# Six small gate and norm operations of a mixture-of-experts block moved from VectorE to GpSimd

## The chip, the core and the metric
One core of one Trainium2 chip. The time is device microseconds for one execution of the kernel; the engines are TensorE (PE), VectorE (DVE), ScalarE (ACT), GpSimd (POOL) and the queue that issues transfers (SP).

## What is computed
A block of three layers over x of 16 sequences x 256 tokens x 128 features, in float32:

```
x = x + 0.5 * moe(layernorm(x))
x = x + attention(layernorm(x))
x = x + 0.5 * moe(layernorm(x))

def moe(x):                       # x: 4096 tokens x 128, 8 experts, top 2
    probs = softmax(x @ Wg)
    top_vals, top_idx = top_k(probs, 2)
    gates = top_vals / sum(top_vals)
    expert_out[e] = x @ We[e] + be[e]
    return sum over the two chosen e of gates * expert_out[e]
```

The attention layer (16 heads of 8 features, causal, with a cumulative log-sigmoid bias) is not touched by the change.

## The kernel before
The 4096 tokens are 32 tiles of 128, kept in SBUF as `x_all` for the whole kernel, in 8 groups of Q = 4 tiles. The kernel runs the first MoE layer over the groups, attention over 16 sequences, and the second MoE layer over the same groups. Each engine has a list of its own, written out by hand as `part(i, s, q)`: i is the step, s its static number, q the place (0 to 3) of a tile inside the group. Step s works on three groups at once: the experts of group s (condition B), the gates of group s + 1 (A) and the norm of group s + 2 (N). Steps from 2 to 5 are a loop on the engines. The last two MoE steps of the first layer and the first three of the second are interleaved with attention steps by a fixed order (`beside`), the same on all engines. Between steps -2, -1 and 0 of the first layer POOL's list has the fills and masks that attention needs (`set_up_rows`, `set_up_columns`, `set_up_masks`). Semaphores order the engines; no instruction overtakes another of its engine.

For a tile, TensorE multiplies by all 8 experts (six matmuls of 512 columns, L416 and L417, since float32 is split into high and low parts). VectorE takes experts 0 to 3 as four chained steps `lower = bank * gate + lower` (`expert`, L288), ScalarE scales experts 4 to 7 (L246, `scaled`), POOL adds them in pairs (L216 `pair`, L220 `upper`, together `add_upper`), and VectorE adds lower and upper into x (`finish`, L297). Two buffers of each alternate between tiles.

The gates of the next group take, in order:
- TensorE: the logits' twelve small matmuls in q = 1.
- VectorE: the largest values (L357) and their difference `gap` (L374), the indices of the two largest (L376).
- ScalarE: `egap` = exp(gap) (L252), followed on its list by four `xn` (L270, the normalised tiles of the group after) and the scaled tile of q = 2.
- VectorE in q = 2: `hot` (L362, which expert is the first and second choice), `denom` (L366), `g12` (L380, L396), and `hot` times `g12` (L401).
- VectorE in q = 3: `gates` (L369, sum of the two), `gates3` (L383 and L388, high and low parts).
- TensorE in q = 0 of the next step, behind its experts: transpose of `gates3` (L434); ScalarE copies it (L259, ahead of its scaled tile); TensorE multiplies it with the bias (L441); VectorE adds that to x (L340).

The norm of a group takes VectorE's L335 and L344 (`moments`), `neg_mean` (L352) and `var_eps` (L353), in q = 0, with L315 and L316 as the same two for the first two groups; then POOL's `rstd_of`: `rstd` = var_eps to the power -1/2 (L225) and `shift` (L228), behind `add_upper` of q = 0.

`chain` is a semaphore that counts VectorE's gate steps, CH of them a group; `after_link(n, k)` waits for step k.

Of the kernel before, what the change touches and what calls it, by code (L numbers as in the profile page):

```python
# [4 lines left out]
FP32 = mybir.dt.float32  # L5
# [3 lines left out]
ALU = mybir.AluOpType  # L9
# [3 lines left out]
P = 128  # L13
EPS = 1e-5
# [10 lines left out]
def wait_apart(eng, sem, value, counted):  # L25

    eng.wait_ge(sem, value)
    eng.sem_inc(counted, 1)
# [137 lines left out]
def moe_layer(nc, ctx, c, made, tiles, banks, x_all, tag, x_dram=None, out_dram=None, before=None):  # L166
# [30 lines left out]
    CH = 8  # L197
# [14 lines left out]
    def gpsimd(pool):  # L212
# [10 lines left out]
        def rstd_of(n, b):  # L223
            pool.wait_ge(eps_done, n)
            nc.gpsimd.tensor_tensor(rstd[:, b], var_eps[:, b], c["minus_half"][:, 0:Q],  # L225
                                    ALU.pow).then_inc(rstd_done, 1)
            pool.wait_ge(rstd_done, n)
            nc.gpsimd.tensor_tensor(shift[:, b], neg_mean[:, b], rstd[:, b], ALU.mult).then_inc(shift_done, 1)  # L228

        def part(i, s, q):  # L230
            N, B, b, n = s + 2 < G, 0 <= s, s % 2, i + 3
            if B:
                add_upper(i, q)
            if q == 0 and N and not (x_dram is not None and s == -1):
                rstd_of(n, b)
            if q == 0 and x_dram is not None and s == -2:
                rstd_of(2, 1)
# [39 lines left out]
    def vector(dve):  # L277
# [21 lines left out]
        def after_link(n, k):  # L299

            dve.wait_ge(chain, (n - 1) * CH + k)

        def first_groups():

            for g in range(2):
# [9 lines left out]
                nc.vector.tensor_scalar(neg_mean[:, g], moments[:, g, :, 0], -1.0, None, ALU.mult)  # L315
                nc.vector.tensor_scalar(var_eps[:, g], moments[:, g, :, 1], EPS, None, ALU.add).then_inc(eps_done, 1)  # L316

        def part(i, s, q):
            N, A, B = s + 2 < G, -1 <= s and s + 1 < G, 0 <= s
            a, b, m, n = (s + 1) % 2, s % 2, i + 3, i + 2  # L320
            flat = gates[:, a].rearrange("p q e -> p (q e)")
# [28 lines left out]
            if q == 0 and N and not early:  # L350
                dve.wait_ge(mom_done, m)
                nc.vector.tensor_scalar(neg_mean[:, b], moments[:, b, :, 0], -1.0, None, ALU.mult)  # L352
                nc.vector.tensor_scalar(var_eps[:, b], moments[:, b, :, 1], EPS, None, ALU.add).then_inc(eps_done, 1)  # L353
# [5 lines left out]
            if q == 2 and A:  # L359

                dve.wait_ge(no_ready, n)
                nc.vector.tensor_tensor(hot[:, :, :, :], every, best_no[:, :, 0:2].rearrange("p q r -> p r q").unsqueeze(3)  # L362
                                        .broadcast_to([P, 2, Q, E]), ALU.is_equal)

                dve.wait_ge(egap_ready, n)
                nc.vector.tensor_scalar(denom[:, :], egap[:, :], 2.0, 2.0, ALU.mult, ALU.add).then_inc(chain, 1)  # L366
            if q == 3 and A:
                after_link(n, 6)
                nc.vector.tensor_tensor(gates[:, a], hot[:, 0], hot[:, 1], ALU.add).then_inc(chain, 1)  # L369
# [11 lines left out]
            if q == 3 and A:  # L381
                after_link(n, 7)
                nc.vector.tensor_copy(gates3[:, 0:3:2], flat.unsqueeze(1).broadcast_to([P, 2, Q * E])).then_inc(chain, 1)  # L383
            if B:
                expert(i, s, q, 2)
            if q == 3 and A:
                after_link(n, 8)
                nc.vector.tensor_tensor(gates3[:, 1], flat, gates3[:, 0].bitcast(FP32), ALU.subtract).then_inc(gates_ready, 1)  # L388
# [10 lines left out]
            if q == 2 and A:  # L399
                after_link(n, 5)  # L400
                nc.vector.tensor_tensor(hot[:, :, :, :], hot[:, :, :, :],  # L401
                                        g12[:, :, :].unsqueeze(3).broadcast_to([P, 2, Q, E]), ALU.mult).then_inc(chain, 1)
# [676 lines left out]
```

## Time and profile before

| | |
|---|---|
| median of 3 runs | 488.97 us (486.0 to 489.73) |
| the profiled execution | 487.24 us, span from first to last instruction 485.5 us |
| TensorE matmul busy | 416.7 us (86%) |
| VectorE busy | 372.5 us (77%) |
| ScalarE busy | 278.3 us (57%) |
| POOL busy | 239.7 us (49%) |
| mean granted TensorE clock | 0.981 |

Busy time is what an engine's instructions took, without their waits; matmuls are pipelined, so a busy TensorE is not one at its peak. Shares are averages over the three layers: the first MoE layer lies at about 16 to 100 us, attention at about 80 to 405 us, the second MoE layer from about 375 us on. "Start" in the rows below is in us from the first instruction, L is the line of the kernel, and a bracket tells how long the engine was idle before and what released it.

### The profile page before, as it was taken

The page shows a single profiled execution, that of the slowest core. Times are in us where ns is not written, and L with a number is a line of the kernel's source. Part 1 is how long each engine was busy: PE and PEld are TensorE (multiplying, and loading weights), DVE is VectorE, ACT ScalarE, POOL GpSimd, SP SyncE. Part 2 cuts the span into 40 slices and gives each one's busy share as a digit, 9 for nine tenths or more (in the row PEclk, how much of TensorE's full clock was granted, in tenths as well). Part 3 has the DMA queues.
Part 4 walks back from the last instruction along what each step waited for, and adds up shares of the span by engine and source line. Part 5 has one row for each costly group of instructions (what it writes and reads, how often), then busy time and mean ns, then how long its engine had stood idle before and what let it go on. Part 6 is the DMA issues. An engine that isn't in the chain of part 4 may idle for free.

```text
span 485.5 us, 12085 instructions
## 1 busy us (share of the span) xinstructions
PE 416.7 (86%) x3472; PEld 303.6 (63%) x3488; DVE 372.5 (77%) x1316; ACT 278.3 (57%) x758; POOL 239.7 (49%) x397
## 2 busy tenths in 40 slices
PE   1888887847799999999999999999989999888884
PEld 0656566526556766676676676676667666566662
DVE  4999999874856865876785686676576658999995
ACT  5676766440354555565556466455555685666753
POOL 8955566351425534533543543553442543566554
PEclk9999999895989999999999999999999999999999
DMA  3311000033333333234233233323322000001101
GB/s 108 92 52 20 1 0 1 8 99 109 101 98 101 94 100 115 73 96 114 69 104 102 85 96 100 100 84 98 111 77 80 4 3 0 24 24 32 33 22 43
DMA packets 29402, 32.47 MB, mean 67 GB/s; under 512 B 2312, under 2 KB 26140, under 8 KB 29370
## 3 DMA queue, kind: packets, MB, share of 16 engines
q1 hardware_dynamic: 28282, 31.57, 22.1%
q10 hardware_dynamic: 1088, 0.52, 0.4%
q8 instruction: 14, 0.23, 0.2%
q14 instruction: 18, 0.15, 0.1%
HBM read 16.05 MB, written 15.20 MB: 64 GB/s over the span
## 4 chain that ended last, share of the span: by engine, by line
PE 40%; DVE 22%; DMA 19%; issue 10%; ACT 3%; POOL 3%; DVEq 1%; SPq 1%; ACTq 0%; POOLq 0%; another core or an unknown queue 0%
DMA a_q_rows<-a_max_t 16%; PE bank L847 10%; PE bank L862 7%; DVE m_lower L288 7%; PE bank L877 6%; PE bank L850 3%; PE bank L968 2%; PE bank L960 2%; PE bank L963 2%; DVE m_stats L335 2%; DMA q_stage<-a_q_parts 2%; POOL m_pair L216 2%; DVE x_all L297 2%; DVE m_best_no L376 2%; PE bank L886 1%
## 5 line engine op out<-in xcount | busy, mean ns | idle before, releaser
L773 DVE TENSOR_REDUCE a_neg_max<-bank 128x2 f32<-128x512 f32 (+1 forms) x192 | 124.3, 687 | 76.2 <-PE bank L850 70.2
L712 ACT ACTIVATE a_weights<-bank 128x512 f32<-128x512 f32 x192 | 108.4, 592 | 60.5 <-PE bank L862 55.6
L658 POOL TENSOR_SCALAR_AFFINE_SELECT a_weights<-a_weights 128x512 f32<-128x512 f32 (+1 forms) x96 | 75.7, 790 | 127.9 <-ACT a_weights L712 127.7
L847 PE MATMUL bank<-a_k_rows,a_q_rows 104*128 104x256 f32 (+1 forms) x512 | 100.9, 321 | 7.7 <-DMA a_k_rows<-k_stage 6.5
L847 PEld LDWEIGHTS bank<-a_k_rows,a_q_rows 104*128 104x128 f32 x512 | 78.9, 199 | 26.9 <-issue 18.5
L246 ACT ACTIVATE m_scaled<-bank,m_gates 128x128 f32<-128x128 f32 x256 | 72.6, 367 | 25.0 <-PE bank L417 25.0
L862 PE MATMUL bank<-a_q_rows,a_k_rows 106*128 106x512 f32 (+1 forms) x192 | 69.8, 442 | 11.1 <-DMA a_q_rows<-a_max_t 10.5
L216 POOL TENSOR_TENSOR m_pair<-m_scaled 128x256 f32<-128x256 f32 x64 | 48.3, 755 | 60.4 <-ACT m_scaled L246 60.1
L288 DVE SCALAR_TENSOR_TENSOR m_lower<-bank,m_gates,m_lower 128x128 f32<-128x128 f32 x192 | 66.1, 344 | 1.2
L877 PE MATMUL bank<-a_weights,a_v 128*32 128x128 f32 x1536 | 61.6, 279 | 0.0
L850 PE MATMUL bank<-a_mask,a_ident 128*128 128x256 bf16 (+1 forms) x176 | 56.4, 321 | 0.0
L877 PEld LDWEIGHTS bank<-a_weights,a_v 128*32 128x32 f32 x1536 | 36.1, 109 | 25.4 <-issue 20.6
L416 PE MATMUL bank<-we_hi,m_xt_hi 128*128 128x512 f32 x64 | 31.8, 497 | 13.7 <-DVE m_lower L288 13.6
L862 PEld LDWEIGHTS bank<-a_q_rows,a_k_rows 106*128 106x128 f32 (+1 forms) x192 | 29.9, 193 | 17.2 <-DMA a_q_rows<-a_max_t 10.0
L701 ACT ACTIVATE a_max_t<-bank 32x128 fp32r<-32x128 f32 x32 | 8.5, 267 | 46.7 <-PE bank L891 46.7
L220 POOL TENSOR_TENSOR m_upper<-m_pair 128x128 f32<-128x128 f32 x64 | 29.6, 462 | 5.7 <-POOL m_pair L216 1.3
L416 PEld LDWEIGHTS bank<-we_hi,m_xt_hi 128*128 128x128 f32 x64 | 12.4, 194 | 24.0 <-DVE m_lower L288 23.3
L270 ACT ACTIVATE m_xn<-x_all,m_shift,m_rstd 128x128 f32<-128x128 f32 (+1 forms) x64 | 26.4, 486 | 0.3 <-POOL m_shift L228 0.3
L417 PE MATMUL bank<-we_hi,m_xt_hi 128*128 128x512 f32 x64 | 25.8, 403 | 0.0
L417 PE MATMUL bank<-we_lo,m_xt_hi 128*128 128x512 f32 x64 | 25.8, 403 | 0.0
L416 PE MATMUL bank<-we_lo,m_xt_hi 128*128 128x512 f32 x64 | 25.7, 402 | 0.0
L417 PE MATMUL bank<-we_hi,m_xt_lo 128*128 128x512 f32 x64 | 25.7, 402 | 0.0
(126 smaller groups left out, 784.0 us busy)
## 6 DMA issues: line engine op xcount, KB each, us to landing
a_k_rows<-k_stage SPq DMA_DIRECT2D x16, 416.0 KB
k_stage<-a_k_parts SPq DMA_DIRECT2D x48, 128.0 KB
q_stage<-a_q_parts SPq DMA_DIRECT2D x48, 128.0 KB
a_q_rows<-q_stage SPq DMA_DIRECT2D x64, 96.0 KB
x_all<-in_L_attn_x SPq DMA_DIRECT2D x8, 256.0 KB, 2.8
out_x<-x_all SPq DMA_DIRECT2D x8, 256.0 KB, 2.3
we<-in_L_ffn_We SPq DMA_DIRECT2D x1, 512.0 KB, 4.0
k_stage<-a_c_parts SPq DMA_DIRECT2D x32, 16.0 KB
```

The costliest lines, as they stand in the source:

```text
L216: nc.gpsimd.tensor_tensor(pair[:, q % 2], scaled[:, q % 2, 0:2], scaled[:, q % 2, 2:4], ALU.add).then_inc(pair_done, 1)
L246: last = nc.scalar.activation(scaled[:, q % 2, j], y_high[q % 2][:, j * D:(j + 1) * D], ACT.Copy, scale=gates[:, s % 2, q, 4 + j:5 + j])
L288: nc.vector.scalar_tensor_tensor(out=lower[:, q % 2, j], in0=y_low[q % 2][:, j * D:(j + 1) * D], scalar=gates[:, s % 2, q, j:j + 1], in1=t ...
L416: nc.tensor.matmul(y_low[q % 2][:, :], x_part, w_part[:, 0:H], start=k == 0, stop=k == 2)
L417: last = nc.tensor.matmul(y_high[q % 2][:, :], x_part, w_part[:, H:2 * H], start=k == 0, stop=k == 2)
L658: nc.gpsimd.affine_select(out=diagonal, in_=diagonal, compare_op=ALU.is_ge, fill=0.0, base=0, pattern=[[0, heads.stop - heads.start], [1, P]],
L712: nc.scalar.activation(weights[n // 2 % 3][:, half:half + 4, :].rearrange("p h n -> p (h n)"), wt_bank[n % 2][:, :], ACT.Exp).then_inc(wt_ ...
L773: nc.vector.tensor_reduce(neg_max[:, t, first:first + heads], score_bank[p % 2][:, :].rearrange("p (h n) -> p h n", h=heads), AX.X, ALU.ma ...
L847: nc.tensor.matmul(bank[:, n * keys:(n + 1) * keys], q_rows[b][0:KR, h, t * P:(t + 1) * P], k_rows[b][0:KR, h % NU, 0:keys], start=n == 0, ...
L850: nc.tensor.matmul(own, ident16[:, :], mask16[:, 0:heads, :], start=False, stop=True, skip_group_check=True).then_inc(scores_ready, 1)
L862: nc.tensor.matmul(bank[:, :], k_rows[b][0:rows, u, jt * P:(jt + 1) * P], q_rows[b][0:rows, u:H:NU, t * P:(t + 1) * P], start=True, stop=T ...
L877: last = nc.tensor.matmul(out_bank[t][32 * g:32 * (g + 1), u // 2 * P:(u // 2 + 1) * P], v_sb[b][:, jt * H // 2 + 2 * g + u // 2, u % 2:u ...
```

## The change
POOL takes six operations from VectorE: `var_eps` and `neg_mean` of the norm (at the head of `rstd_of`), and `hot` times `g12`, the sum of `gates`, and the two steps of `gates3`. The four of the gates stand in POOL's list in q = 3, ahead of `add_upper` of that tile. The copy in L383 becomes an addition of 0.0. New semaphores carry the dependencies: `hot_done` from VectorE to POOL, `hot_scaled`, `gates_done` and `gates_hi_done` between POOL's steps, `neg_done` for the norm; VectorE's writing of `hot` waits for `gates_done` of the group before. L315 and L316, for the first two groups, are moved too.

```diff
--- before.py
+++ after.py
@@ -194,7 +194,9 @@
     y_ready, high_used = sem("y_ready"), sem("high_used")
     low_chain, pair_done, upper_done, upper_used = sem("low_chain"), sem("pair_done"), sem("upper_done"), sem("upper_used")
     stored, waited = sem("stored"), sem("waited")
-    CH = 8
+    neg_done, hot_done, hot_scaled = sem("neg_done"), sem("hot_done"), sem("hot_scaled")
+    gates_done, gates_hi_done, pool_waited = sem("gates_done"), sem("gates_hi_done"), sem("pool_waited")
+    CH = 5
 
     def load_group(sp, g):
 
@@ -221,14 +223,32 @@
                                     ALU.add).then_inc(upper_done, 1)
 
         def rstd_of(n, b):
+            wait_apart(pool, mom_done, n, pool_waited)
+            nc.gpsimd.tensor_scalar(var_eps[:, b], moments[:, b, :, 1], EPS, None, ALU.add).then_inc(eps_done, 1)
+            nc.gpsimd.tensor_scalar(neg_mean[:, b], moments[:, b, :, 0], -1.0, None, ALU.mult).then_inc(neg_done, 1)
             pool.wait_ge(eps_done, n)
             nc.gpsimd.tensor_tensor(rstd[:, b], var_eps[:, b], c["minus_half"][:, 0:Q],
                                     ALU.pow).then_inc(rstd_done, 1)
+            pool.wait_ge(neg_done, n)
             pool.wait_ge(rstd_done, n)
             nc.gpsimd.tensor_tensor(shift[:, b], neg_mean[:, b], rstd[:, b], ALU.mult).then_inc(shift_done, 1)
 
         def part(i, s, q):
             N, B, b, n = s + 2 < G, 0 <= s, s % 2, i + 3
+            A, a, m = -1 <= s and s + 1 < G, (s + 1) % 2, i + 2
+            flat = gates[:, a].rearrange("p q e -> p (q e)")
+            if q == 3 and A:
+                pool.wait_ge(hot_done, m)
+                pool.wait_ge(chain, (m - 1) * CH + 5)
+                nc.gpsimd.tensor_tensor(hot[:, :, :, :], hot[:, :, :, :],
+                                        g12[:, :, :].unsqueeze(3).broadcast_to([P, 2, Q, E]), ALU.mult).then_inc(hot_scaled, 1)
+                pool.wait_ge(hot_scaled, m)
+                nc.gpsimd.tensor_tensor(gates[:, a], hot[:, 0], hot[:, 1], ALU.add).then_inc(gates_done, 1)
+                wait_apart(pool, gates_done, m, pool_waited)
+                nc.gpsimd.tensor_scalar(gates3[:, 0:3:2], flat.unsqueeze(1).broadcast_to([P, 2, Q * E]), 0.0, None,
+                                        ALU.add).then_inc(gates_hi_done, 1)
+                pool.wait_ge(gates_hi_done, m)
+                nc.gpsimd.tensor_tensor(gates3[:, 1], flat, gates3[:, 0].bitcast(FP32), ALU.subtract).then_inc(gates_ready, 1)
             if B:
                 add_upper(i, q)
             if q == 0 and N and not (x_dram is not None and s == -1):
@@ -312,13 +332,10 @@
                     last = nc.vector.bn_aggr(moments[:, g, k], stats[:, k])
                 last.then_inc(mom_done, 1)
                 dve.wait_ge(mom_done, g + 1)
-                nc.vector.tensor_scalar(neg_mean[:, g], moments[:, g, :, 0], -1.0, None, ALU.mult)
-                nc.vector.tensor_scalar(var_eps[:, g], moments[:, g, :, 1], EPS, None, ALU.add).then_inc(eps_done, 1)
 
         def part(i, s, q):
             N, A, B = s + 2 < G, -1 <= s and s + 1 < G, 0 <= s
             a, b, m, n = (s + 1) % 2, s % 2, i + 3, i + 2
-            flat = gates[:, a].rearrange("p q e -> p (q e)")
             early = x_dram is not None and s < 0
 
             if early and s == -2 and q == 0:
@@ -347,10 +364,6 @@
                 if q == 0:
                     dve.wait_ge(bias_added, i + 1)
                 expert(i, s, q, 0)
-            if q == 0 and N and not early:
-                dve.wait_ge(mom_done, m)
-                nc.vector.tensor_scalar(neg_mean[:, b], moments[:, b, :, 0], -1.0, None, ALU.mult)
-                nc.vector.tensor_scalar(var_eps[:, b], moments[:, b, :, 1], EPS, None, ALU.add).then_inc(eps_done, 1)
             if q == 1 and A:
                 wait_apart(dve, logits_ready, n, waited)
                 for k in range(Q):
@@ -359,14 +372,12 @@
             if q == 2 and A:
 
                 dve.wait_ge(no_ready, n)
+                at_least(dve, gates_done, n - 1)
                 nc.vector.tensor_tensor(hot[:, :, :, :], every, best_no[:, :, 0:2].rearrange("p q r -> p r q").unsqueeze(3)
-                                        .broadcast_to([P, 2, Q, E]), ALU.is_equal)
+                                        .broadcast_to([P, 2, Q, E]), ALU.is_equal).then_inc(hot_done, 1)
 
                 dve.wait_ge(egap_ready, n)
                 nc.vector.tensor_scalar(denom[:, :], egap[:, :], 2.0, 2.0, ALU.mult, ALU.add).then_inc(chain, 1)
-            if q == 3 and A:
-                after_link(n, 6)
-                nc.vector.tensor_tensor(gates[:, a], hot[:, 0], hot[:, 1], ALU.add).then_inc(chain, 1)
             if B:
                 expert(i, s, q, 1)
             if q == 1 and A:
@@ -378,14 +389,8 @@
             if q == 2 and A:
                 after_link(n, 3)
                 nc.vector.reciprocal(g12[:, 0], denom[:, :]).then_inc(chain, 1)
-            if q == 3 and A:
-                after_link(n, 7)
-                nc.vector.tensor_copy(gates3[:, 0:3:2], flat.unsqueeze(1).broadcast_to([P, 2, Q * E])).then_inc(chain, 1)
             if B:
                 expert(i, s, q, 2)
-            if q == 3 and A:
-                after_link(n, 8)
-                nc.vector.tensor_tensor(gates3[:, 1], flat, gates3[:, 0].bitcast(FP32), ALU.subtract).then_inc(gates_ready, 1)
             if q == 3 and N:
                 dve.wait_ge(hi_ready, m)
                 nc.vector.tensor_tensor(xt_lo[:, b], xt_bank[:, :], xt_hi[:, b].bitcast(FP32), ALU.subtract).then_inc(lo_ready, 1)
@@ -396,10 +401,6 @@
                 nc.vector.tensor_tensor(g12[:, 1], egap[:, :], g12[:, 0], ALU.mult).then_inc(chain, 1)
             if B:
                 expert(i, s, q, 3)
-            if q == 2 and A:
-                after_link(n, 5)
-                nc.vector.tensor_tensor(hot[:, :, :, :], hot[:, :, :, :],
-                                        g12[:, :, :].unsqueeze(3).broadcast_to([P, 2, Q, E]), ALU.mult).then_inc(chain, 1)
             if q == 3 and s == G - 1:
                 finish(G * Q - 1, 1)
         return part
```

## Rows read from the trace of the kernel before

**Rows 1.** Stretch by engine: us, busy us (instructions), TensorE clock, DMA share, GB/s
```profile
440.00:450.00 10.00, 8.57 (x42) 6.46 (x42) 9.88 (x54) 6.85 (x24) 6.06 (x10) 1.00 0.09 26
```

**Rows 2.** VectorE in order of time (start us, us), fourth tile of a steady group
```profile
441.52 0.22 DVE L401 TENSOR_TENSOR m_hot<-m_hot,m_g 128x64 f32<-128x64 f32 x1
441.83 0.35 DVE L288 SCALAR_TENSOR_TENSOR m_lower<-bank,m_gates,x_all 128x128 f32<-128x128 f32 x1
442.09 0.34 DVE L369 TENSOR_TENSOR m_gates<-m_hot 128x32 f32<-128x32 f32 x1
442.36 0.34 DVE L288 SCALAR_TENSOR_TENSOR m_lower<-bank,m_gates,m_lower 128x128 f32<-128x128 f32 x1
442.62 0.36 DVE L383 CAST m_gates<-m_gates 128x64 fp32r<-128x64 f32 x1
442.90 0.34 DVE L288 SCALAR_TENSOR_TENSOR m_lower<-bank,m_gates,m_lower 128x128 f32<-128x128 f32 x1
443.16 0.17 DVE L388 TENSOR_TENSOR m_gates<-m_gates 128x32 fp32r<-128x32 f32 x1
443.26 0.68 DVE L391 TENSOR_TENSOR m_xt_lo<-bank,m_xt_hi 128x512 fp32r<-128x512 f32 x1
```

**Rows 3.** Weight loads in order of time, the gates' transpose [idle before, releaser]
```profile
443.39 0.12 PEld L434 LDWEIGHTS bank<-ident,m_gates 128*96 128x96 f32 x1 [0.31 <-DVE m_gates L388]
```

**Rows 4.** In order of time, from the logits' largest values: VectorE, ScalarE, POOL
```profile
437.87 0.39 DVE L357 MAX8 m_best<-bank 128x8 f32<-128x8 f32 x4
...
438.90 1.66 ACT L270 ACTIVATE m_xn<-x_all,m_shift,m_rstd 128x128 f32 x4
440.46 1.11 ACT L246 ACTIVATE m_scaled<-bank,m_gates 128x128 f32<-128x128 f32 x4
...
441.65 0.73 POOL L216 TENSOR_TENSOR m_pair<-m_scaled 128x256 f32<-128x256 f32 x1 [2.45 <-ACT m_scaled L246]
442.46 0.47 POOL L220 TENSOR_TENSOR m_upper<-m_pair 128x128 f32<-128x128 f32 x1
```

**Rows 5.** VectorE in order of time, two groups later, where it waits for TensorE
```profile
463.32 0.18 DVE L388 TENSOR_TENSOR m_gates<-m_gates 128x32 fp32r<-128x32 f32 x1
...
464.77 0.69 DVE L340 TENSOR_TENSOR x_all<-x_all,bank 128x512 f32<-128x512 f32 x1 [0.21 <-PE bank L441]
...
467.66 0.39 DVE L357 MAX8 m_best<-bank 128x8 f32<-128x8 f32 x4 [0.32 <-PE bank L449]
```

**Rows 6.** VectorE and POOL in order of time, first tile of a steady group
```profile
445.97 0.32 DVE L288 SCALAR_TENSOR_TENSOR m_lower<-bank,m_gates,x_all 128x128 f32<-128x128 f32 x1
446.21 0.40 DVE L352 TENSOR_SCALAR m_neg_mean<-m_moments 128x4 f32<-128x4 f32 x1
446.52 0.16 DVE L353 TENSOR_SCALAR m_var_eps<-m_moments 128x4 f32<-128x4 f32 x1
446.59 0.72 DVE L288 SCALAR_TENSOR_TENSOR m_lower<-bank,m_gates,m_lower 128x128 f32<-128x128 f32 x2
...
446.12 0.46 POOL L220 TENSOR_TENSOR m_upper<-m_pair 128x128 f32<-128x128 f32 x1 [0.16 <-POOL m_pair L216]
```

**Rows 7.** Groups of POOL instructions: count, busy us, mean ns, idle before, releaser
```profile
L225 POOL TENSOR_TENSOR m_rstd<-m_var_eps,minus_half 128x4 f32<-128x4 f32 x16 | 17.3, 1082 | 3.6 <-DVE m_var_eps L353 2.4 <-DVE m_var_eps L316 1.1
L228 POOL TENSOR_TENSOR m_shift<-m_neg_mean,m_rstd 128x4 f32<-128x4 f32 x16 | 3.2, 200 | 1.3
```

**Rows 8.** In order of time at the start of the kernel: POOL, VectorE, ScalarE
```profile
16.69 0.94 POOL L630 MEMSET a_ones_r<- 2x1024 f32 x1
...
20.62 0.63 POOL L648 TENSOR_SCALAR_AFFINE_SELECT a_mask<-a_mask 128x512 bf16<-128x512 bf16 x1
...
17.91 0.16 DVE L396 TENSOR_TENSOR m_g<-m_egap,m_g 128x4 f32<-128x4 f32 x1
...
24.73 1.64 ACT L270 ACTIVATE m_xn<-x_all,m_shift,m_rstd 128x128 f32<-128x128 f32 x4
```

**Rows 9.** VectorE in order of time, where the second MoE part begins beside attention
```profile
376.05 0.92 DVE L352 TENSOR_SCALAR m_neg_mean<-m_moments 128x4 f32<-128x4 f32 x1
```

## The prediction
> **What bounds the kernel now.** I read the busy shares first, then one stretch of the second MoE part, then the order of time inside one group, engine by engine, and last the first and last group and the seams with attention. Over the whole span TensorE is the busiest engine, an average that hides stages with different limits. Inside a MoE part VectorE is busy 9.88 of 10 us, TensorE 8.57 and POOL 6.06 at a full clock [rows 1], so a group of four tiles goes at VectorE's pace. The interval between groups is that between two L388: 463.32 - 443.16 = 20.16 us for two groups, 10.08 each, taken as 10.1 [rows 2, 5]. Each MoE part has one group at its start, six further gate computations in a row before or beside attention, and ten plain steady intervals in all (five a part).
>
> The question is not how much VectorE loses but what the gates hang on once POOL makes them. POOL runs its list in order. In a steady group it waits for ScalarE's scaled tile of the third tile, adds the pair at 441.65 and the upper half at 442.46, which ends at 442.93 [rows 4]. Only behind that does the change put the four gate steps. VectorE today ends them at 443.33 [rows 2], and TensorE waits for them: its weight load for the gates' transpose sat idle 0.31 us until L388 [rows 3]. So there is no slack at all at this end: what POOL delivers later, TensorE starts later.
>
> **What leaves VectorE.** I price by distance between starts, since durations overlap. L288 links wait for the one before and stand 0.38 us apart with nothing between (two of them take 0.72 us: 0.38 + 0.34 [rows 6, 2]). An operation that follows an L288 without needing it starts 0.26 behind it (442.36 to 442.62). L401 needs nothing of its neighbours and is needed by neither: its 441.52 to 441.83, 0.31 us, are all saved [rows 2]. L369: 441.83 to 442.36 is 0.53 against 0.38, saves 0.15. L383: 442.36 to 442.90 is 0.54, saves 0.16. L388: 443.16 to 443.26, saves 0.10 [rows 2]. L352 and L353: 445.97 to 446.59 is 0.62 against 0.38, saves 0.24 [rows 6]. Together 0.96 us a group: if VectorE stayed the limit, 10.1 would become 9.1.
>
> **What comes to POOL.** No row shows a tensor_scalar there. Two-input operations cost 0.20 us at 4 elements a partition [rows 7], 0.47 at 128 and 0.73 at 256 [rows 4], so about 2.1 ns an element over 0.2 or a little less. That gives 0.32 for the product of 64 elements, 0.26 for the sum of 32, 0.26 for the subtraction. The copy of 64 (a tensor_scalar) lies between 0.20 and 0.32; I take 0.25, one input being the nearer to the lower row. They are a chain with three waits on POOL's own results. Such a wait costs 0.08 us between pair and upper (442.38 to 442.46 [rows 4]); with a second semaphore and a counted threshold I take 0.12, bounds 0.08 and 0.2. The chain G is 0.32 + 0.26 + 0.25 + 0.26 + 0.36 = 1.45 us. Its floor, four operations at the 0.20 of the smallest row and three waits of 0.08, is 1.04; its ceiling, each operation held up once, about 2.0. The two norm steps add 0.20 each and their waits, some 0.6 us before rstd.
>
> **The lap that closes.** With the gates on POOL a ring runs through four engines once a group; I add it up from one end of the gates to the next.
> - Gates ready to L340 (transpose, ScalarE's copy, bias matmul): 463.32 + 0.18 = 463.50 to 464.77, where L340 did wait for TensorE: 1.27 us.
> - L340 to L357: 464.77 to 467.66, with L357 waiting for TensorE's logits: 2.89 us. Here the matmuls of one tile and twelve logits matmuls lie, not the two removed norm steps, so VectorE's saving doesn't shorten it [rows 5].
> - L357 to the end of the third tile's upper half: 437.87 (the largest values), 438.90 (four xn, behind the exponential of the gap), 440.46 (scaled tile), 441.65, 442.46, end 442.93: 5.06 [rows 4], and 0.05 to POOL's next step: 5.11 us. xn cannot start before the gap is known, as ScalarE's list has them in that order, and the scaled tile stands behind xn.
> - G, 1.45 us.
> The lap is 1.27 + 2.89 + 5.11 + 1.45 = 10.72 us, over the 10.1 of today and the 9.1 that VectorE would allow. So VectorE gives 0.96 back into idle time, mostly before L340, and each steady interval becomes 0.62 us longer: ten of them, +6.2. Even at the floor of G the lap is 10.31, +0.2 each. The norm steps lie on a branch: upper half of the first tile, norm 1.9 (0.6, rstd 1.02 to 1.08, shift 0.20, the rest waits [rows 7]), xn. By POOL's pairs behind the gates I reckon xn could start 4.9 to 5.1 us after the gates by this branch, and 5.2 by the lap above, so they cost nothing as long as G stays about where I put it; without that cover they cost their 0.6.
>
> **The ends.** At the start POOL has a long list of fills (L630 at 16.69 to L648's end at 21.25, 4.56 us) [rows 8]. They stand behind the group's fourth-tile place in POOL's list, where nothing of POOL stood until now; the gates wait for g12 (L396 ends 18.07), so the gates are ready at 19.6, the fills end at 24.2, pair and upper of the first tile at 25.5, norm at 27.4, and xn starts at 27.4 to 27.5 instead of 24.73 [rows 8]: +2.7. The next gates come behind POOL's upper half, 1.5 instead of 0.4 after it [rows 2, 4]: +1.1. Together +3.8, bounds +1 (the fills then hidden) and +5. In the second MoE the first gates are late by the same step, +0.9 (0.7 to 1.1), five intervals are in the ten, and the last, without xn in its lap, I put at +0.3. At the seams with attention VectorE is relieved: L352 took 0.92 us beside a POOL operation just ahead of a row maximum [rows 9], so -0.7 there (0 to -1.4), and -0.3 (0 to -1.0) beside the first attention steps. Attention itself, some 260 us, contains no moved instruction: 0.
>
> Sum: 3.8 + 6.2 + 0.9 + 0.3 - 0.7 - 0.3 = +10.2 us. Against the profiled execution's own 487.24 us (its span is 485.5) that is 497.4; that execution lies 1.7 us under the median of the three runs, 488.97, which would give 499.2. I take a value between the two, 498.
>
> **A rule beside the rows.** L352 took 0.40 us at 446.21 against 0.16 for its like L353, and ended at 446.61, with POOL's L220 that ended at 446.58; at the seam it took 0.92 [rows 6, 9]. The Trainium skill, "SBUF — State Buffer", section "Who interferes with whom", says that VectorE operations in a two-port mode, or with two inputs in SBUF, and POOL operations exclude one another for a whole instruction. The trace agrees. By that rule the change removes such collisions from VectorE and hands POOL four to six more operations that can be held up; the first is in my start-to-start prices, the second is the third rival.
>
> **Rivals.**
> - VectorE stays the limit and the chain is hidden: ten intervals of -0.96 and -1.0 at the seams give 476.6 us. For it speaks the 98% of VectorE. Against it, POOL ends the upper half at 442.93, and TensorE wants the gates at about 443.3: a chain of over 0.4 us is already late. It would need ScalarE to finish the scaled tile a full microsecond earlier in the group. It decides from a lap below 10.1, thus G under 0.83, where the floor is 1.04. Chance 0.1.
> - Chain at its floor, and the fills not on the path: ten times +0.2, +0.9, +0.3, -1.0, and +1 to +3 for the start: 489.5 to 492, within 1%. For it: small operations might all cost 0.20. Chance 0.18.
> - The lap lengthened by collisions: each POOL step of the chain and of the norm held up by 0.24, as L352 was; G 2.4 with the chain's four, lap 11.7, ten times +1.6 and the ends: about 507. Against: during the chain VectorE mostly reads PSUM (L288, L391). Chance 0.1.
> - My forecast, G between 1.2 and 2.0: chance 0.62, 494 to 503.
>
> **Range and chances.** A measurement of this kernel can tell a change from none from about 1%. The range 490 to 504 takes in the forecast and most of the second rival; outside stay the first, the third in part. Faster by over 1%: 0.1, the first rival. Within 1%: 0.2, the second rival and a little of the forecast's lower end. Slower by over 1%: 0.7.
>
> **What would show it.** In the changed kernel: six groups of VectorE gone and 96 POOL operations of 0.20 to 0.33 us new; gate groups 10.7 us apart; VectorE under 90% busy in a MoE stretch with idle time before L340, put down to TensorE's bias matmul; TensorE waiting for POOL's gates, no longer for VectorE's; xn of the first full group near 27 us. It is wrong if groups stand under 10.1 apart, if POOL's chain takes under 1 us, or if the fills don't delay the first pair. A granted TensorE clock that falls in MoE stretches with more idle time would lengthen the 2.89 us and make it worse than forecast.

## The result, and the profile after

The changed kernel takes 499.34 us (median of 4 runs, 497.43 to 507.1) beside 487.49 for the kernel before (4 runs, 483.54 to 489.73); the ratio is 1.024, 95% interval 1.018 to 1.030. It is slower, by 1.8 to 3.0%. One of its four runs, 507.1 us with a mean granted TensorE clock of 0.939 where the others have 0.964 to 0.984, is left out of the ratio. The profiled execution took 497.83 us, its span is 496.1 against 485.5, so 10.6 us are to be found.

The stretch of one group in the second MoE part of the changed kernel (us, busy time of TensorE, its weight loads, VectorE, ScalarE, POOL with the instructions, clock, transfers) answers to [rows 1]:

```profile
441.90:452.70 10.80, 8.63 (x42) 6.52 (x42) 9.31 (x49) 6.96 (x23) 7.50 (x17) 1.00 0.09 27
```

TensorE's work is the same and its clock is full, VectorE is down from 99% to 86%, POOL up from 61% to 69%, and the group takes 10.8 instead of 10.1 us. No engine is as busy as VectorE was before; the time goes in waits. POOL in order of time, behind ScalarE's third tile, and then TensorE's first instruction that needs the gates (answers to [rows 3, 4]):

```profile
449.87 0.74 POOL L218 TENSOR_TENSOR m_pair<-m_scaled 128x256 f32<-128x256 f32 x1 [1.66 <-ACT m_scaled L266]
450.69 0.47 POOL L222 TENSOR_TENSOR m_upper<-m_pair 128x128 f32<-128x128 f32 x1
451.12 0.29 POOL L243 TENSOR_TENSOR m_hot<-m_hot,m_g 128x64 f32<-128x64 f32 x1
451.49 0.25 POOL L246 TENSOR_TENSOR m_gates<-m_hot 128x32 f32<-128x32 f32 x1
451.93 0.39 POOL L248 TENSOR_SCALAR m_gates<-m_gates 128x64 fp32r<-128x64 f32 x1 [0.20 <-POOL m_gates L246]
452.40 0.25 POOL L251 TENSOR_TENSOR m_gates<-m_gates 128x32 fp32r<-128x32 f32 x1
...
452.71 0.32 PE L435 MATMUL bank<-ident,m_gates 128*96 128x128 f32 x1 [1.06 <-POOL m_gates L251]
```

Product, sum, copy and subtraction run from 451.12 to 452.65, 1.53 us, and TensorE stood idle 1.06 us until the last of them. In the same kernel VectorE and ScalarE close the lap (answers to [rows 4, 5]):

```profile
443.27 0.69 DVE L357 TENSOR_TENSOR x_all<-x_all,bank 128x512 f32 x1 [1.11 <-PE bank L442]
445.90 0.39 DVE L370 MAX8 m_best<-bank 128x8 f32<-128x8 f32 x4
...
446.65 0.21 ACT L272 ACTIVATE m_egap<-m_gap 128x4 f32<-128x4 f32 x1 [0.95 <-DVE m_gap L385]
447.13 1.65 ACT L290 ACTIVATE m_xn<-x_all,m_shift,m_rstd 128x128 f32 x4 [0.28 <-POOL m_shift L234]
```

VectorE's relief shows as 1.11 us idle ahead of the bias addition. With the gates before this group ready at 441.89, the lap is 1.38 (to L357) + 2.63 (to L370) + 5.22 (to POOL's product) + 1.53 = 10.76 us. The last bracket matters for the path: ScalarE had its exponential done at 446.86 and could have begun `xn`, but POOL's `shift` ended only at 447.00. So it is in nine of the ten steady groups: `shift` ends 5.00 to 5.12 us after the gates, the exponential 4.96 to 5.10, and `xn` starts 0.1 to 0.3 us behind the exponential. The lap closes through POOL's norm.

At the start of the kernel (answers to [rows 8]) the last of attention's fills ends at 24.31 instead of 21.25, and ScalarE's xn waits 2.27 us for POOL:

```profile
23.69 0.62 POOL L649 TENSOR_SCALAR_AFFINE_SELECT a_mask<-a_mask 128x512 bf16<-128x512 bf16 x1
24.40 0.74 POOL L218 TENSOR_TENSOR m_pair<-m_scaled 128x256 f32<-128x256 f32 x1
...
27.67 1.65 ACT L290 ACTIVATE m_xn<-x_all,m_shift,m_rstd 128x128 f32<-128x128 f32 x4 [2.27 <-POOL m_shift L234]
```

Where the 10.6 us arise, by the lateness of the same event after and before (the end of the last gate step of a group, VectorE's addition of attention's output, its scan):

| stretch | lateness at its end | gained or lost | forecast |
|---|---|---|---|
| start, to the second gates (33.19 against 29.18) | 4.01 | +4.0 | +3.8 |
| five intervals, first MoE | 7.21 | +3.2 | +3.1 |
| beside attention's first step, to its scan | 4.83 | -2.4 | -0.3 |
| attention, to its 14th sequence (392.87 against 387.76) | 5.11 | +0.3 | 0 |
| beside attention's end, to the second MoE's second gates | 7.54 | +2.4 | +0.2 |
| five intervals, second MoE | 10.68 | +3.1 | +3.1 |
| last interval and tail | 10.6 | -0.1 | +0.3 |

### The profile page after: what moved, and what is told of

Same layout as the page of the kernel before. It is cut to its first block, busy times and chain, and to the rows that moved or that the text cites. A ratio compares the mean times of both kernels' runs of the same rounds, so it can differ in the third digit from the quotient of the medians.

```text
span 496.1 us, 12153 instructions
## 1 busy us (share of the span) xinstructions
PE 421.4 (85%) x3488; PEld 307.6 (62%) x3488; DVE 356.9 (72%) x1220; ACT 278.9 (56%) x758; POOL 263.2 (53%) x493
## 4 chain that ended last, share of the span: by engine, by line
PE 42%; POOL 18%; DMA 17%; issue 11%; ACT 5%; DVE 4%; SPq 1%; POOLq 1%; ACTq 0%; DVEq 0%
DMA a_q_rows<-a_max_t 14%; PE bank L848 10%; PE bank L863 8%; POOL m_pair L218 6%; PE bank L878 6%; PE bank L851 5%; POOL m_upper L222 3%; POOL m_rstd L230 3%; ACT m_scaled L266 2%; PE bank L969 2%; PE bank L964 2%; PE bank L961 2%; DMA q_stage<-a_q_parts 2%; PE bank L887 1%; PE bank L965 1%
## 5 line engine op out<-in xcount | busy, mean ns | idle before, releaser
L848 PE MATMUL bank<-a_k_rows,a_q_rows 104*128 104x256 f32 (+1 forms) x512 | 102.6, 326 | 6.1 <-DMA a_k_rows<-k_stage 5.0
L848 PEld LDWEIGHTS bank<-a_k_rows,a_q_rows 104*128 104x128 f32 x512 | 81.1, 203 | 24.7 <-issue 17.0
L863 PE MATMUL bank<-a_q_rows,a_k_rows 106*128 106x512 f32 (+1 forms) x192 | 71.4, 452 | 10.3 <-DMA a_q_rows<-a_max_t 9.6
L218 POOL TENSOR_TENSOR m_pair<-m_scaled 128x256 f32<-128x256 f32 x64 | 47.1, 736 | 42.4 <-ACT m_scaled L266 42.3
L308 DVE SCALAR_TENSOR_TENSOR m_lower<-bank,m_gates,m_lower 128x128 f32<-128x128 f32 x192 | 66.2, 345 | 2.8 <-issue 0.2
L851 PE MATMUL bank<-a_mask,a_ident 128*128 128x256 bf16 (+1 forms) x192 | 64.1, 334 | 0.0
L417 PE MATMUL bank<-we_hi,m_xt_hi 128*128 128x512 f32 x64 | 30.8, 482 | 11.6 <-DVE m_lower L308 11.0
L418 PE MATMUL bank<-we_hi,m_xt_hi 128*128 128x512 f32 x64 | 25.8, 403 | 0.0
L417 PE MATMUL bank<-we_hi,m_xt_lo 128*128 128x512 f32 x64 | 25.7, 402 | 0.0
L418 PE MATMUL bank<-we_hi,m_xt_lo 128*128 128x512 f32 x64 | 25.5, 399 | 0.0
```

The lines of the kernel that those rows point to most:

```text
L218: nc.gpsimd.tensor_tensor(pair[:, q % 2], scaled[:, q % 2, 0:2], scaled[:, q % 2, 2:4], ALU.add).then_inc(pair_done, 1)
L308: nc.vector.scalar_tensor_tensor(out=lower[:, q % 2, j], in0=y_low[q % 2][:, j * D:(j + 1) * D], scalar=gates[:, s % 2, q, j:j + 1], in1=t ...
L417: nc.tensor.matmul(y_low[q % 2][:, :], x_part, w_part[:, 0:H], start=k == 0, stop=k == 2)
L418: last = nc.tensor.matmul(y_high[q % 2][:, :], x_part, w_part[:, H:2 * H], start=k == 0, stop=k == 2)
L848: nc.tensor.matmul(bank[:, n * keys:(n + 1) * keys], q_rows[b][0:KR, h, t * P:(t + 1) * P], k_rows[b][0:KR, h % NU, 0:keys], start=n == 0, ...
L851: nc.tensor.matmul(own, ident16[:, :], mask16[:, 0:heads, :], start=False, stop=True, skip_group_check=True).then_inc(scores_ready, 1)
```

## The experiments

An "interval" below is the time between the ends of the last gate step of two groups in a row. The kernel before has 10.07 to 10.15 us in the second MoE (9.94 to 10.45 in the first), the changed kernel 10.75 to 10.80, with 10.55 for its first (10.57 to 10.98 in the first MoE). Runs sent together share their runs of the kernel before (medians 486.88, 487.02 and 486.35 us). Diffs are against the changed kernel where nothing else is said.

**One half of the change at a time.** Against the kernel before, the norm alone:

```diff
         def rstd_of(n, b):
+            wait_apart(pool, mom_done, n, pool_waited)
+            nc.gpsimd.tensor_scalar(var_eps[:, b], moments[:, b, :, 1], EPS, None, ALU.add).then_inc(eps_done, 1)
+            nc.gpsimd.tensor_scalar(neg_mean[:, b], moments[:, b, :, 0], -1.0, None, ALU.mult).then_inc(neg_done, 1)
             pool.wait_ge(eps_done, n)
...
-                nc.vector.tensor_scalar(neg_mean[:, b], moments[:, b, :, 0], -1.0, None, ALU.mult)
-                nc.vector.tensor_scalar(var_eps[:, b], moments[:, b, :, 1], EPS, None, ALU.add).then_inc(eps_done, 1)
```

> Only the two norm steps are on POOL; the four gate steps stay on VectorE. Theory (the ring through POOL's gates sets the group's interval): without the gates there is no ring, VectorE is again the limit and has lost 0.24 us a group, so groups stand 9.8 to 10.0 us apart, and the kernel is within 3 us of the kernel before, on either side. Rival (the norm steps on POOL are what costs, since ScalarE's xn waited for POOL's shift in the changed kernel): groups stand over 10.3 apart and the kernel is 4 us or more slower than before.

486.29 us, ratio 1.0005 (0.996 to 1.005). In the second MoE intervals of 9.92 to 9.94 us alternate with ones of 10.43 to 10.64; in the first only one of five is long, 10.67; 9.8 to 10.0 was expected of all. In the long ones a VectorE sum with two SBUF inputs sits out a POOL operation; VectorE and POOL in order of time:

```profile
59.60 0.79 DVE L302 TENSOR_TENSOR x_all<-m_lower,m_upper 128x128 f32 x1
...
59.51 0.72 POOL L217 TENSOR_TENSOR m_pair<-m_scaled 128x256 f32<-128x256 f32 x1 [0.85 <-ACT m_scaled L251]
```

The sum takes 0.79 us where 0.28 is usual, and ends (60.39) behind the pair (60.23). In each long interval `gap`, a difference on 4 elements, is held up in the same way (0.58 to 0.60 us, else 0.15). VectorE's 0.24 us are gained in some groups and lost again in others. Without the gates on POOL the norm costs nothing in total.

The four gate steps alone (the reverse diff on the changed kernel):

> Only the four gate steps are on POOL; the norm steps stay on VectorE. Theory (ring): intervals of 10.5 to 10.75 us, at most 0.25 less than the changed kernel's 10.77, and a time within 3 us of it. Rival (norm): intervals back at 10.1 and the time at most 3 us above the kernel before.

497.41 us, ratio 1.023 (1.019 to 1.028): all of the loss. Intervals 10.67 to 11.15, mostly 10.87, a tenth of a microsecond more than with the norm on POOL too, where the expectation had 10.5 to 10.75. The trace shows a collision as the reason. Here `shift` ends 4.4 us after the gates and holds nobody up, but VectorE's `gap`, on which the exponential and then `xn` depend, takes 0.26 to 0.55 us in the steady groups instead of 0.15:

```profile
467.88 0.55 DVE L387 TENSOR_TENSOR m_gap<-m_best 128x4 f32<-128x4 f32 x1
```

It ends at 468.43, just behind POOL's pair sum (467.66 to 468.40). The norm steps on POOL thus hold `xn` back by up to 0.28 us in the changed kernel and at the same time push that pair sum out of the way of `gap`; what is left is the tenth.

**The same steps at another place.**

```diff
-            if q == 3 and A:
+            if q == 2 and A:
                 pool.wait_ge(hot_done, m)
                 pool.wait_ge(chain, (m - 1) * CH + 5)
```

> The changed kernel with POOL's four gate steps ahead of the pair sum of the group's third tile instead of the fourth, so they no longer stand behind ScalarE's scaled tile of that place. Theory (ring): what costs is the place and not the engine. The ring then runs from the gap over g12 to the gates, about 1 us shorter; intervals of 9.3 to 9.7 us, and 8 to 14 us less than the changed kernel, thus faster than the kernel before by some us, the fills at the start still costing. Rival (POOL's own load, or the delay of the third tile's pair that now stands behind the gates): intervals stay at 10.3 or more.

505.58 us, ratio 1.036 (1.026 to 1.045): slower still, intervals of 11.03 to 11.12, one of 11.34. My theory as I had applied it fell here, and the rival about the third tile's pair held. POOL, VectorE and TensorE in order of time:

```profile
63.95 0.74 POOL L218 TENSOR_TENSOR m_pair<-m_scaled 128x256 f32<-128x256 f32 x1
64.77 0.45 POOL L222 TENSOR_TENSOR m_upper<-m_pair 128x128 f32<-128x128 f32 x1
...
65.34 0.71 DVE L317 TENSOR_TENSOR x_all<-m_lower,m_upper 128x128 f32 x1 [0.75 <-POOL m_upper L222]
...
66.38 0.50 PE L417 MATMUL bank<-we_hi,m_xt_hi 128*128 128x512 f32 x1 [0.78 <-DVE m_lower L308]
```

The gates are early enough now (ready at 64.00), but the upper half of the third tile comes behind them; VectorE's `finish` waits 0.75 us for it and then takes 0.71 us instead of 0.28, ending just behind POOL's next pair sum (65.91), the last L308 of the fourth tile stands behind `finish`, and TensorE waits 0.78 us for the bank that this L308 frees. It is a ring again, through another product of POOL. It does not take away that the late place costs; it shows that the chain of 1.5 us costs at either. The collision is in every group here (`finish` 0.71 to 0.80 us), and how much of the loss is its own wasn't tried.

**The chain longer and shorter.**

```diff
+                nc.gpsimd.tensor_tensor(spare[:, :, :], hot[:, 0], hot[:, 1], ALU.add).then_inc(spare_done, 1)
+                pool.wait_ge(spare_done, m)
                 nc.gpsimd.tensor_tensor(gates[:, a], hot[:, 0], hot[:, 1], ALU.add).then_inc(gates_done, 1)
```

> The changed kernel with one more chained POOL operation (the sum of the gates written once more into a spare tile, then waited for) ahead of the sum of the gates. It adds about 0.25 us and a wait of 0.12. Theory (ring): every group's interval grows by all of it, 0.37 us, from 10.77 to 11.1, and the kernel by 4 to 5 us. Rival (the chain has slack, another wait ends last): intervals grow by under 0.1 us and the time by under 1 us.

511.73 us, ratio 1.054 (1.048 to 1.060): 12.4 us over the changed kernel by the medians, about three times what was forecast. Two neighbouring stretches of it, each one group:

```profile
70.00:82.70 12.70, 11.59 (x42) 9.13 (x42) 9.29 (x46) 7.09 (x23) 7.83 (x18) 0.73 0.00 0
82.70:93.80 11.10, 8.63 (x42) 6.51 (x42) 9.94 (x53) 6.96 (x23) 7.72 (x19) 1.00 0.00 0
```

At the full clock a group takes 11.1 us, as the ring says (+0.33 where 0.37 was forecast). In four of the ten steady intervals the mean granted clock is 0.73 to 0.83, a mix of the levels of 1.2 and 2.4 GHz, and a group takes 12.4 to 13.1. So the time of the whole run holds two costs: ten times 0.33 us for the ring, and the lower clock for most of the rest. That the longer ring brings the lower clock is likely, since the mean over the whole run is 0.931 to 0.943 in all four executions of this kernel, but it isn't shown: a kernel with the changed kernel's ring has one such interval too (below, first gates on VectorE).

```diff
-                nc.gpsimd.tensor_tensor(hot[:, :, :, :], hot[:, :, :, :],
+            if q == 2 and A:
+                nc.vector.tensor_tensor(hot[:, :, :, :], hot[:, :, :, :],
                                         g12[:, :, :].unsqueeze(3).broadcast_to([P, 2, Q, E]), ALU.mult).then_inc(hot_scaled, 1)
```

> The changed kernel with the product of hot and g12 back on VectorE, three gate steps left on POOL. Theory (ring through POOL's gates): the chain is 0.30 us and a wait of 0.08 shorter, intervals of 10.3 to 10.45 us instead of 10.77, and 4 us less. Rival (norm branch and gates' branch are equal, so that shortening one gives less): intervals of 10.6 or more.

496.28 us, ratio 1.018 (1.010 to 1.026). Intervals of 10.37 to 10.45 (10.17 for the first of the second MoE), 0.38 under the changed kernel's: the whole link, product and wait. Between three, four and five links the interval follows the chain at 10.39, 10.76 and 11.1, as a ring must. The time fell by 3 us by the medians; forecast 4. The intervals of the two ratios overlap, so it is the trace that shows it.

**The start.** First with attention's fills cut in four pieces (the two of ones ahead of the first gates, the others behind steps -1, 0 and 1):

> The changed kernel with attention's fills and masks on POOL cut in four pieces: the first ahead of the first gates, where POOL waits, the others behind steps -1, 0 and 1. Theory (the fills stood behind the first gates and held up the first pair, norm and xn): xn of the first full group starts near 25.2 instead of 27.67 us, the next gates are ready near 31 instead of 33.19, the later intervals stay at 10.8, and the kernel is 1.5 to 3 us faster than the changed one. Rival (the start is hidden behind another wait): the time changes by under 1 us.

499.42 us, ratio 1.026 (1.022 to 1.030), no gain. The first pair did start earlier, at 21.98 instead of 24.40, but xn only at 27.30 instead of 27.67: in this execution the first full group's second tile of matmuls stood 0.43 us apart where the changed kernel has 0.235, thus at the lower clock level, and the logits were late. The pieces behind steps 0 and 1 cost 0.4 and 0.5 us in the next two intervals (10.93 and 11.43 for 10.57 and 10.98). It doesn't decide. The cleaner trial leaves the fills whole and makes the first group's gates on VectorE:

```diff
-            if q == 3 and A:
+            if q == 3 and A and not (x_dram is not None and s == -1):
                 pool.wait_ge(hot_done, m)
```

> The changed kernel, but the gates of the very first group are made on VectorE with the same four steps, so that attention's fills on POOL start as early as in the kernel before. Theory (the fills behind the first gates cost at the start): POOL's first pair at 21.3 to 21.8 instead of 24.4, xn of the first full group at 24.9 to 25.3 instead of 27.67, the next gates ready near 30.7 instead of 33.19, later intervals unchanged at 10.8, 2 to 3 us less in all. Rival (TensorE's clock or another wait holds the start): the next gates at 32 or later.

496.89 us, ratio 1.021 (1.015 to 1.027), 2.5 us under the changed kernel by the medians, though the intervals of the two ratios overlap. In the trace the place is plain: pair at 21.73, xn at 25.02, the next gates at 30.55 instead of 33.19, 2.6 us, all as the fills' order says. Later in the same execution it was all lost again: an interval of 12.80 us from 62.84 on, at a mean granted clock of 0.60, and one of 11.32 behind it (the changed kernel has 10.79 and 10.75), so that the seventh gates end at 86.96 against 87.04.

**What VectorE's relief is worth.** Against the kernel before:

> The kernel before with the six operations left out altogether (gates, gates3, the negated mean and the variance with eps are constants filled once, so gates and norm are not computed; everything else runs). It shows what VectorE's relief is worth when nothing is added to POOL. Theory of the prediction (VectorE's pace, 0.96 us a group): intervals of 9.1 to 9.2. Rival (the hand-over of two expert banks between TensorE and VectorE, seen where VectorE waited for TensorE's matmuls of the fourth tile with two steps moved): intervals of 9.5 or more, half of the relief at most.

483.31 us, ratio 0.994 (0.990 to 0.998). The bias additions of the steady groups stand 9.70 to 9.80 us apart, 9.75 in the mean, where the kernel before has 10.09, so 0.34 us a group is all that VectorE's 0.96 are worth, with nothing put on POOL. (TensorE's transpose waits for `g12` alone in this kernel, so the figure is a ceiling.) Where the rest stays shows in a kernel told of below (two early steps, fills cut in pieces); TensorE's first matmul of the fourth tile and VectorE's first step with it:

```profile
453.08 0.50 PE L419 MATMUL bank<-we_hi,m_xt_hi 128*128 128x512 f32 x1 [0.60 <-DVE m_lower L297]
...
454.90 0.35 DVE L297 SCALAR_TENSOR_TENSOR m_lower<-bank,m_gates,x_all 128x128 f32<-128x128 f32 x1 [0.23 <-PE bank L420]
```

TensorE may start the fourth tile when VectorE has freed the second tile's bank, needs 1.8 us for its matmuls, and VectorE waits for them. What VectorE saves in between is idle time; the kernel with six steps left out shows the same wait of 0.22 us.

**Fewer steps, at the place where POOL waits.** Against the kernel before, product and sum on POOL in q == 2:

```diff
+            if q == 2 and A:
+                pool.wait_ge(hot_done, m)
+                pool.wait_ge(chain, (m - 1) * CH + 5)
+                nc.gpsimd.tensor_tensor(hot[:, :, :, :], hot[:, :, :, :],
+                                        g12[:, :, :].unsqueeze(3).broadcast_to([P, 2, Q, E]), ALU.mult).then_inc(hot_scaled, 1)
+                pool.wait_ge(hot_scaled, m)
+                nc.gpsimd.tensor_tensor(gates[:, a], hot[:, 0], hot[:, 1], ALU.add).then_inc(gates_done, 1)
             if B:
                 add_upper(i, q)
```

> From the kernel before: only two steps of the gates, the product with g12 and the sum, are on POOL, ahead of the pair sum of the third tile, where POOL waits for ScalarE; the two steps of gates3 and the norm stay on VectorE. The moved chain is 0.67 us instead of 1.55, so it ends about when ScalarE's tile is there and the third tile's upper half is late by under 0.5 us. Theory (what costs is a chain longer than POOL's waiting time at its place): no ring, VectorE is the limit less 0.46 us a group, intervals of 9.6 to 9.8 and 3 to 5 us less than before, less 1 to 2 at the start where the fills are moved back. Rival (any gate step on POOL costs, as in the four early ones): intervals of 10.2 or more and a kernel slower than before.

491.22 us, ratio 1.008 (1.003 to 1.012), intervals 10.07 to 10.4 in the second MoE. Neither expectation: no ring, but no gain, the kernel is 0.3 to 1.2% slower. VectorE's relief before the fourth tile is the idle time just seen (read from the trace, not tried by itself), and in the intervals of 10.35 us and more a `finish` takes 0.78 to 0.82 us instead of 0.28.

> The kernel of the two early steps with the fills cut in pieces. Theory (fills at the start cost on top): 1 to 2 us less than with the fills in one piece, 4 to 6 us under the kernel before. Rival (the start is hidden): the same as with one piece within 0.5 us.

490.41 us, ratio 1.007 (1.004 to 1.011): no different from the one before, and not the 4 to 6 us under the kernel before that were expected.

> As the one before, and the two norm steps on POOL too. Theory (VectorE is the limit, 0.24 us less a group): intervals of 9.4 to 9.6, 2 us less. Rival (collisions of VectorE's operations of two SBUF inputs with POOL's, and POOL's norm before xn, take it back, as when the norm alone was moved): the same time within 1 us, with some VectorE sums of lower and upper at 0.7 us instead of 0.28.

491.26 us, ratio 1.010 (1.007 to 1.013). Intervals of 9.82 to 9.84 us, 0.25 under the kernel before, which is what the norm steps of the first tile were priced at, but 10.4 to 10.8 in the two ahead of them in each MoE, and a start delayed by the lower clock as with the spread fills above (matmuls of the first full group 0.43 us apart, the second gates at 32.44 instead of 29.18).

> Product and sum of the gates on POOL ahead of the third tile's pair, the norm steps on POOL, the first group's product and sum on VectorE, the fills where they were in the kernel before. Theory (with a short chain at a place where POOL waits, and the start undisturbed, VectorE's relief shows): intervals of 9.82 us, start within 0.6 us of the kernel before, in all 1 to 3 us faster than before. Rival (the seams with attention and collisions take it): no faster than the kernel before.

489.62 us, ratio 1.005 (1.001 to 1.010). The start is undisturbed (xn at 25.07), intervals 9.83, but again two of 10.45 to 10.79 at the head of each MoE. It isn't faster. The four long intervals show the collisions again: in each, a `finish` takes 0.47 to 0.82 us instead of 0.28 and `gap` 0.37 to 0.62 instead of 0.15 (one `gap` ends at 428.91, just behind POOL's pair sum at 428.88), while in the intervals of 9.83 they take at most 0.39 and 0.16. Why the first two groups of each MoE meet POOL there and the later ones don't stays open. No version that computes the gates beats the kernel before.

## Why the prediction was right, and where not

498 us was forecast, 499.34 measured, inside the range, with the sign. The main term, ten intervals made longer by a ring through POOL's gates, held in kind and size. One branch of the lap was taken for covered and was not, both seams were mis-sized, and the total is as near as it is partly by luck.

*The ring.* Right in mechanism, shown by moving the two halves of the change apart and by chains of three, four and five links. Size: 10.72 forecast, 10.76 measured. Term by term 1.27 became 1.38, 2.89 became 2.63, 5.11 became 5.22, G of 1.45 became 1.53. The largest miss inside G is the copy: 0.39 us where I took 0.25, outside my bounds of 0.20 to 0.32, as I had put a one-input operation under a two-input one of its size. The waits were 0.08, 0.19 and 0.08.

*L340 to L357.* I argued that the removed norm steps don't shorten this part as TensorE's logits end last. The conclusion holds, the reason doesn't. In the steady group VectorE did not wait for the logits, and the part takes 2.63. With the two steps back on VectorE (gates alone moved) it takes 2.63 too (464.69 to 467.32): there they take 0.16 us each and fit between the chained L308. The 2.85 that steady groups of the kernel before have come with `neg_mean` held up by POOL (0.40 for 0.16). So the 0.24 us priced for the norm steps was that collision's. The row that I took 2.89 from came from a group without norm, at the end.

*The norm costs nothing.* This step failed, by a little. The branches were forecast at 4.9 to 5.1 us from gates to xn through the norm, against 5.2 through the gap. Measured, the exponential of the gap ends 4.97 us after the gates and shift 5.11, and xn starts at 5.24: the norm branch is the one that closes the lap, and ScalarE waited 0.28 us for it. That 5.24 is so near to 5.2 is luck, since the route that I had added up was shorter by 0.2 and the wait that I had put at nothing filled the gap. It costs less than it seems, as without it `gap` runs into POOL's pair sum and the interval is 0.1 longer (gates alone moved).

*The start.* Forecast +3.8, measured +4.0, and the first group's gates on VectorE give 2.6 of it back against the 2.7 forecast for the fills.

*The seams.* Both were mis-sized, in opposite directions, and the sum is near only because they cancel, which is luck. Beside attention's first step -2.4 instead of -0.3: from the seventh gates to attention's scan the changed kernel takes 12.77 us, and so do four others with the late gates (gates alone, fills cut, one link less, first gates on VectorE: 12.76 to 12.77); the longer chain takes 14.6, the kernel before 15.14, the norm alone 15.23. In the one TensorE is at the full clock there, in the other not (before, then after):

```profile
84.00:88.00 4.00, 2.69 (x8) 2.21 (x9) 3.42 (x22) 0.48 (x2) 1.09 (x2) 0.60 0.00 0
```

```profile
88.00:92.00 4.00, 3.73 (x24) 3.24 (x24) 3.59 (x15) 1.88 (x7) 3.10 (x6) 1.00 0.00 0
...
401.00:405.00 4.00, 3.98 (x24) 2.27 (x24) 1.19 (x5) 2.83 (x7) 1.27 (x2) 0.59 0.03 6
```

Over that whole stretch of the kernel before, 15.14 us, the mean granted clock is 0.89, so the clock can have cost at most 1.7 us of it (an estimate, 0.11 of 15.14), and the rest of the 2.4 is the order of work. The kernels with two early steps point the same way: 15.0 and 15.1 us at a mean clock of 0.89 with the norm on VectorE, 13.8 twice at 1.00 with the norm on POOL. The two weren't tried apart. At the other seam I forecast -0.7 for L352's collision and +0.9 for the first gates; measured +1.8 up to attention's last addition but one and +0.6 behind it. The time between attention's second and third last addition tells why: 11.76 us before, 11.73 with the gates alone moved, 12.06 with the norm alone, 13.57 in the changed kernel and 14.65 with one link less. The norm steps on POOL cost 0.3 there (with the norm alone moved xn waits 0.29 us for the shift, ahead of attention's exponentials). The other 1.5 goes with the clock of 0.59 in the row above, which not every execution has, so it is a matter of the execution that was profiled: two others with the moved norm and gates, the fills cut and the first gates on VectorE, took 12.06 and 12.08.

*The rivals.* "VectorE stays the limit" was priced at 0.96 us a group. Even with its condition met it would have given 0.34: the ceiling of that rival was wrong by more than half, since I took the distance between VectorE's starts for time on the path. The rival at the floor has a slip in its sum: its own terms, 2 + 0.9 + 0.3 - 1.0 and 1 to 3, give 490.4 to 492.4 us and not 489.5 to 492. The rival of collisions was right that they cost and wrong about whom: it was VectorE's `finish` and `gap` that sat out operations of POOL's, while POOL's chain was never lengthened: product and sum were at 0.29 to 0.30 and 0.25 in every group.

## What to carry to other kernels

An engine at 99% isn't proof that each microsecond taken from it is one gained: leave the steps out and see what the ceiling is, before moving them. When steps move to another engine, add up the lap from their result back to their own start; here everything followed from what stood in front of them on POOL's list, and the lap of 10.7 against 10.1 was readable beforehand. Where the lap has two branches that come out within a few tenths of each other, add up both: here the one put down as covered ended last. An engine that waits 2.4 us has room for a chain of that length only if its next product isn't wanted sooner: four steps early were worse than four late.

## What the runs showed of the hardware that was not expected

- POOL's tensor_scalar on 64 elements a partition from float32 took 0.39 us, more than its two-input product of the same size, 0.29; on 4 elements 0.23 against 0.20 for a product.
- VectorE's difference on 4 elements a partition (`gap`) took 0.15 us by itself and up to 0.62 beside a POOL sum of 256, ending 0.03 us behind it in the two places read (468.43 and 468.40, 428.91 and 428.88). Moving operations between these two engines shifts those that stay against each other, and one such meeting held `gap` up by 0.4 us.
- In the kernel with one POOL link of 0.33 us more, TensorE's granted clock fell in four of ten steady intervals (means of 0.73 to 0.83), at 1.3 to 2 us each; in the traced execution of the changed kernel it is 1.00 in all ten. That link cost the kernel 12 us, of which its own length explains 3.3. One of ten steady intervals of the kernel with its first gates on VectorE, whose ring is no longer than the changed kernel's, had the lower clock as well, so the length of the ring isn't all of it.
